# Node stage of a four-layer graph network: the row means leave two products with gamma

## The chip, the cores and the metric

The kernel runs on one core of one Trainium2 chip. The metric is the time of one execution on the device, in microseconds; the median of three runs is shown below. Engines are named as the profile names them: PE (TensorE), DVE (VectorE), ACT (ScalarE), POOL (GpSimd), SP (SyncE).

## What is computed

50,000 nodes with 128 features go through four layers, each followed by a residual and a layer norm. Edges (25,000) are sorted by their destination. What bears on this change is the dense work that every node gets, edge or no edge. In the first layer a node without edges only sees itself, so its row is

```python
out = x @ W + bias
f = gelu(out)
f = (f - mean(f)) / sqrt(var(f) + 1e-5) * gamma + beta     # gamma, beta: L0
x1 = layernorm(x + (f + x))
```

and in the third layer (L2) a node without incoming edges has no message, so that

```python
h = x2 + bo                                                # x2: a layer-normed row
h = (h - mean(h)) / sqrt(var(h) + 1e-5) * gamma + beta     # gamma, beta: L2
x3 = layernorm(x2 + h)
```

All of it is float32. Nodes with edges are computed again in later stages ("hops") and written over the others.

## The kernel before, in words

The program is a row of stages with a barrier of all engines between them. Setup loads the weights and derives small tables. Then comes the **node stage**, which the change is about: it takes all nodes through the layers as if they had no edges. After it come the marks of the edges' ends, the hops of the four layers, and a copy of the result.

The node stage takes 1,024 nodes per iteration: 49 chunks, and 57 turns of a loop over `t`, since a chunk is worked on over eight turns (software pipelining). Chunk `t` is loaded, turned, multiplied with `W0` and gone through gelu; chunk `t-1` gets its first layer norm and residual; `t-2` its second norm; `t-3` the second layer's three products; `t-4` and `t-5` the third norm; `t-6` and `t-7` the third layer. Tiles are 128 partitions wide and hold 8 rows of 128 features per partition (128x1024), worked on in two halves (`h` = 0 and 1, four rows of 128 each, 128x512). The same turn also takes 512 edges' end points through a gather (POOL), two turns on PE and a store.

Each engine runs its own list of instructions, in the order in which the code is written, and waits on semaphores; there is no scheduler. So what a wait holds up is everything written behind it on its engine. Names that matter:

- `gelu(c, h)` on ACT (L604) writes `gT[h]`, the gelu rows with the features on the partitions. `turn_g(c, h)` on PE turns them by `turn` (L368, four transposes with `ident`) into the PSUM tiles `T_G[h]`, rows on the partitions.
- DVE takes statistics of a row by `bn_stats` (L694, "stats"), two rows to an instruction. Once per turn a **batch** of ten small instructions (L716 to L769, tiles of 40 columns) makes from all rows' variances the factors `rs` = 1/sqrt(var + eps) and `nm` = -mean * rs, for the five norms at once. Its last (L769) signals `scaled`.
- Between the batch's small instructions lie the wide ones: L719 adds a bias to `xw_b[2]`, the last tile that ACT copies in a turn (L686, signal `xw2`); L724, L732, L767 and the stats of the third norm follow.
- Behind `scaled`, DVE works on the first norm: L782 makes `a_b = (T_G - mean) * gamma0`, one instruction for each of the 8 rows, since the mean is a number per partition and row; L786 makes `t_b = a_b * rs + t_b`, again a row at a time. Then the stats of `t_b`; L794 `hd_b = x2 + bo` and its stats; stats of `T_G[0]`; L804 makes `d_b = (hd_b - mean) * gamma2` in 8 instructions and L808 `s_b = d_b * rs + s_b` in 8; stats of `s_b` and of `T_G[1]`.
- ACT waits for `scaled` at its L626 and then runs its three sets of eight `apply` instructions (L594, 128x128 each, for the second, third and fifth norm), two gelus, four relus and the copies out of PSUM, down to L686.

The lines of DVE around the change:

```python
V.scalar_tensor_tensor(out=blocks(a_b)(4 * h + k), in0=blocks(T_G[h])(k), scalar=mean[:, LNA, 4 * h + k:4 * h + k + 1],
                       in1=gamma0[:], op0=ALU.subtract, op1=ALU.mult).then_inc(S("ag"), 1)
...
V.scalar_tensor_tensor(out=blocks(d_b)(k), in0=blocks(hd_b[q % 2])(k), scalar=mean[:, LND, k:k + 1],
                       in1=gamma2[:], op0=ALU.subtract, op1=ALU.mult).then_inc(S("dg"), 1)
```

Of the kernel before, what the change touches and what calls it, by code (L numbers as in the profile page):

```python
# [47 lines left out]
def build(nc, x, src, dst, ea32, ea64, ew, w, out):  # L48
# [3 lines left out]
    def sb(name, shape, dt=F32):  # L52
        return ctx.enter_context(nc.sbuf_tensor(name, shape, dt))
# [43 lines left out]


    ident = sb("ident", [P, P])
    ones = sb("ones", [1, P])  # L100
    eps = sb("eps", [P, 1])
    W0 = sb("W0", [P, D])
# [41 lines left out]
    with ExitStack() as tmp:  # L144
# [7 lines left out]
        att = tb("att", [P, 2, D])  # L152
        prod = tb("prod", [P, 4, D])
        sums = tb("sums", [P, 6, 4])
        Win, WinT, Ws0 = tb("Win", [P, D]), tb("WinT", [P, D]), tb("Ws0", [P, D])
        b_in_rep = tb("b_in_rep", [P, P])
        b_in, bs0c = tb("b_in", [P, 1]), tb("bs0c", [P, 1])
# [28 lines left out]
        with nc.Block() as block:  # L186
# [66 lines left out]
            @block.vector  # L253
            def _(v):
                V = nc.vector
                v.wait_ge(pool_dma["edges"], 64)
                V.tensor_copy(edge_f[:], edge_i[:]).then_inc(S("edges_f"), 1)
                v.wait_ge(S("edges_f"), 1)

                V.tensor_tensor(mark[:, :, 0, :], edge_f[:, :, 1, :], edge_f[:, :, 3, :], ALU.is_equal).then_inc(S("m"), 1)  # L260
                V.tensor_tensor(mark[:, :, 1, :], edge_f[:, :, 1, :], edge_f[:, :, 2, :], ALU.is_equal).then_inc(S("m"), 1)
                v.wait_ge(S("m"), 2)
                V.tensor_scalar(mark[:, :, 4, :], mark[:, :, 0, :], float(FAR), None, ALU.mult).then_inc(S("m"), 1)
                V.tensor_scalar(mark[:, :, 2, :], mark[:, :, 1, :], 0.5, 2 * BIG / 2, ALU.subtract, ALU.mult).then_inc(S("marks"), 1)
                v.wait_ge(S("m"), 3)
                V.tensor_tensor(mark[:, :, 3, :], mark[:, :, 4, :], edge_f[:, :, 1, :], ALU.add).then_inc(S("marks"), 1)

                v.wait_ge(S("win_ps"), 1)
                V.tensor_copy(b_in_rep[:], b_in[:, 0:1].to_broadcast([P, P])).then_inc(S("b_rep"), 1)
                v.wait_ge(S("b_rep"), 1)  # L270
                V.tensor_copy(WinT[:], ps[:, 0, 0:P]).then_inc(S("winT"), 1)
                v.wait_ge(S("wi0_ps"), 3)
                V.tensor_copy(xw0_bias[:], ps[:, 5, 0:P])
                V.tensor_copy(WI0[:], ps[:, 0, 128:256])
                V.tensor_tensor(h1_bias[:], ps[:, 0, 384:385], bs0c[:], ALU.add)
                V.tensor_tensor(prod[:, 0, :], W0[:], att[:, 0, :], ALU.mult).then_inc(S("prod"), 1)
                V.tensor_tensor(prod[:, 1, :], W0[:], att[:, 1, :], ALU.mult).then_inc(S("prod"), 1)
                v.wait_ge(S("prod"), 2)
                for k, t in enumerate((prod[:, 0, :], prod[:, 1, :], Wq3[:], Wk3[:])):
                    V.tensor_reduce(sums[:, k, :], t.rearrange("p (h c) -> p h c", h=4), AX.X, ALU.add).then_inc(S("sums"), 1)  # L280
                V.tensor_reduce(We3s[0:64, :], We3[:].rearrange("p (h c) -> p h c", h=4), AX.X, ALU.add).then_inc(S("sums"), 1)
                v.wait_ge(S("sums"), 5)
                V.memset(att_src[:, 4:8], 0.0)
                V.tensor_copy(att_src[:, 0:4], sums[:, 0, :])
                V.tensor_copy(att_dst[:, 0:4], sums[:, 1, :])
                V.tensor_tensor(att_dst[:, 4:8], sums[:, 0, :], sums[:, 1, :], ALU.add)
                V.tensor_copy(q3_cols[:], sums[:, 2, :])
                V.tensor_copy(k3_rep.rearrange("p (h c) -> p h c", h=4), by_row(sums[:, 3, :], 32))
                V.tensor_copy(we3_rep[0:64, :].rearrange("p (h c) -> p h c", h=4),
                              We3s[0:64, :, None].to_broadcast([64, 4, 32]))  # L290
                V.tensor_scalar(we3_rep[64:65, :].rearrange("p (h c) -> p h c", h=4),
                                We3s[64:65, :, None].to_broadcast([1, 4, 32]), float(32.0 ** 0.5), None, ALU.mult)
                V.tensor_copy(we2_rep.rearrange("p (h c) -> p h c", h=8), We2[:, :, None].to_broadcast([33, 8, 16]))

                v.wait_ge(S("cols_ps"), 6)
                v.wait_ge(S("zeros"), 7)
                V.tensor_copy(src_idx[:, 0:TILES], ps[:, 1, 0:TILES])
                V.tensor_copy(dst_idx[:, 0:TILES], ps[:, 2, 0:TILES])
                V.tensor_copy(end_idx[:, 0:TILES], ps[:, 3, 0:TILES])
# [93 lines left out]
    def wide_rows(t):  # L393

        return t.rearrange("p (j f) -> p j f", f=D)
# [5 lines left out]
    with ExitStack() as tmp:  # L401
# [33 lines left out]
        with nc.Block() as block:  # L435
# [66 lines left out]
            def _(pe):  # L502
# [15 lines left out]
                def turn_g(c, h):  # L518
                    pe.wait_ge(S("gelu"), 2 * c + h + 1)
                    if c:  # L520
                        pe.wait_ge(S("ag"), 8 * (c - 1) + 4 * h + 4)
                    turn(pe, T_G[h], gT[h]).then_inc(S("g_ps"), 1)

                def scores(k):
                    pe.wait_ge(S("xsT"), k + 1)
# [163 lines left out]
            def _(v):  # L689
# [14 lines left out]
                v.wait_ge(S("raw"), 2)  # L704
                for t in range(N_CH + 8):
                    of = raw[(t - 1) % 2].rearrange("p n k (r s) -> p (n k r) s", r=2)
                    mean = raw[(t - 1) % 2].rearrange("p n k (r s) -> p n (k r) s", r=2)[:, :, :, 1]
                    r, b = rs[t % 2].rearrange("p n k -> p (n k)"), nm[t % 2].rearrange("p n k -> p (n k)")
                    n0 = 10 * t
                    cw, cv, cw2 = t - 1, t - 4, t - 6  # L710
# [61 lines left out]
                    for h in range(2):  # L772
                        if m:
                            v.wait_ge(S("xw0_ps"), 2 * c + h + 1)
                            if h == 0 and c >= 2:
                                landed(v, "xw0_out", 2, c - 2)
                            V.tensor_tensor(rows4(half(xw_b[0][c % 2], h)), rows4((T_D, T_B)[h]), each_row(xw0_bias), ALU.add).then_inc(S("xw0"), 1)
                        if live(a):
                            v.wait_ge(S("scaled"), t + 1)
                            v.wait_ge(S("w"), a + 1)  # L780
                            for k in range(4):
                                V.scalar_tensor_tensor(out=blocks(a_b)(4 * h + k), in0=blocks(T_G[h])(k), scalar=mean[:, LNA, 4 * h + k:4 * h + k + 1],  # L782
                                                       in1=gamma0[:], op0=ALU.subtract, op1=ALU.mult).then_inc(S("ag"), 1)
                            for k in range(4 * h, 4 * h + 4):
                                v.wait_ge(S("ag"), 8 * a + k + 1)
                                V.scalar_tensor_tensor(out=blocks(t_b[a % 2])(k), in0=blocks(a_b)(k), scalar=rs[t % 2][:, LNA, k:k + 1],  # L786
                                                       in1=blocks(t_b[a % 2])(k), op0=ALU.mult, op1=ALU.add).then_inc(S("t"), 1)
                            if h == 1:
                                v.wait_ge(S("t"), 8 * a + 8)
                                stats(LNB, t, pairs(t_b[a % 2]), 0, 4, "b_st")  # L790
                    if live(t - 5):
                        q = t - 5
                        v.wait_ge(S("x2"), 2 * (q + 1))
                        V.tensor_tensor(wide_rows(hd_b[q % 2][:]), wide_rows(x2_b[q % 3][:]), row_of_all(bo), ALU.add).then_inc(S("hd"), 1)  # L794
                        v.wait_ge(S("hd"), q + 1)
                        stats(LND, t, pairs(hd_b[q % 2]), 0, 4, "d_st")
                    if live(t):
# [2 lines left out]
                    if live(t - 6):  # L800
                        q = t - 6
                        v.wait_ge(S("w2"), q + 1)
                        for k in range(8):
                            V.scalar_tensor_tensor(out=blocks(d_b)(k), in0=blocks(hd_b[q % 2])(k), scalar=mean[:, LND, k:k + 1],  # L804
                                                   in1=gamma2[:], op0=ALU.subtract, op1=ALU.mult).then_inc(S("dg"), 1)
                        for k in range(8):
                            v.wait_ge(S("dg"), 8 * q + k + 1)
                            V.scalar_tensor_tensor(out=blocks(s_b[q % 2])(k), in0=blocks(d_b)(k), scalar=rs[t % 2][:, LND, k:k + 1],  # L808
                                                   in1=blocks(s_b[q % 2])(k), op0=ALU.mult, op1=ALU.add).then_inc(S("s"), 1)
                        v.wait_ge(S("s"), 8 * q + 8)  # L810
                        stats(LNE, t, pairs(s_b[q % 2]), 0, 4, "e_st")
# [1339 lines left out]
```

## Time and profile before

| | us |
|---|---|
| three runs | 4228.57, 4228.95, 4229.52 |
| median | 4228.95 |
| the profiled execution's own time | 4232.34 |
| span of that execution (first to last instruction) | 4230.3 |
| node stage in it, from L769 of the first turn to the next stage | 29.4 to 1285.4 |
| busy in the span: DVE, PE, POOL, ACT | 3478, 2900, 2568, 2509 |
| mean granted TensorE clock, share of 2.4 GHz | 0.738 |

The profile is of one execution. Busy time counts when an engine had an instruction in work; waits on semaphores are not in it. Instructions that follow each other on an engine overlap a little in the trace, so a group of four may span less than four durations; what counts on a path is the distance from start to start. A row of the timeline merges neighbours that are alike: "x8" with its start and the time from the first start to the last end. Square brackets behind a row tell the idle time before it and what ended it.

### The profile page before, as it was taken

The numbers are of one execution on the slowest core, as the hardware profiler recorded it, in microseconds if no ns is written. First come the engines' busy times: TensorE is split into PE (matmuls) and PEld (weight loads), VectorE is DVE, ScalarE is ACT, GpSimd is POOL, SyncE is SP. The second block draws the span as 40 slices with busy tenths as digits, with TensorE's granted clock in tenths as the row PEclk, the third lists the DMA queues.
The fourth block names the chain that finished last, engine by engine and source line by source line (L and its number), as shares of the span: only waits on it lengthen the run. The fifth ranks groups of instructions, "written<-read, shape, count | busy, mean of one in ns | idle before, by whom it ended". The sixth has DMA issues, their size and how long they took to land. (4 is left out here: it accounts for less than half of the span.)

```text
span 4230.3 us, 49000 instructions
## 1 busy us (share of the span) xinstructions
PE 2899.9 (69%) x12128; PEld 1933.6 (46%) x12128; DVE 3478.3 (82%) x8156; ACT 2509.0 (59%) x5535; POOL 2568.4 (61%) x2300
## 2 busy tenths in 40 slices
PE   5877777777742788745465455478888885777775
PEld 3555455554530344444455344345555554444443
DVE  4999999999986888668788699677777785788886
ACT  3777777777751666635545444356666564565555
POOL 6666666666501666167577577587666651666664
PEclk9899999999975777667657655677777785655655
DMA  4887766665534888457667566322222221333331
GB/s 117 182 184 192 188 180 193 183 192 188 174 138 122 253 249 254 150 176 245 220 199 242 196 184 198 94 73 69 64 66 66 69 55 38 102 87 91 91 94 49
DMA packets 390823, 624.83 MB, mean 148 GB/s; under 512 B 125015, under 2 KB 206080, under 8 KB 390542
## 3 DMA queue, kind: packets, MB, share of 16 engines
q1 hardware_dynamic: 320782, 508.68, 40.0%
q0 software_dynamic: 69760, 113.02, 11.4%
q8 instruction: 101, 1.65, 0.2%
q14 instruction: 180, 1.47, 0.1%
HBM read 338.14 MB, written 287.17 MB: 148 GB/s over the span
## 5 line engine op out<-in xcount | busy, mean ns | idle before, releaser
L1563 POOL DMA_INDIRECT gs_g<-table_xw,slot_idx x588 | 616.8, 1049 | 319.5 <-issue 261.9
L886 POOL DMA_INDIRECT gs_t<-table_x,slot_idx x392 | 418.4, 1067 | 302.3 <-issue 198.9
L493 POOL DMA_INDIRECT gs<-x,src_idx x200 | 223.9, 1119 | 292.2 <-DMA xd_rows<-gd 211.0
L368 PE MATMUL ps<-ident,gs_g 128*128 128x128 f32 x588 | 143.4, 391 | 369.1 <-DMA gs_g<-table_xw,slot_idx 369.0
L1258 POOL DMA_INDIRECT slot_idx<-node_map,src_idx x200 | 242.1, 1211 | 196.9 <-DMA slot_idx<-node_map,src_idx 103.6
L481 POOL DMA_INDIRECT node_map<-slot_no,end_idx x200 | 302.6, 1513 | 60.9 <-issue 60.0
L1601 ACT ACTIVATE hT_g<-u_g 128x512 f32<-128x512 f32 x147 | 92.4, 629 | 391.5 <-DVE u_g L1662 391.1
L1828 POOL DMA_INDIRECT out<-x_t,end_idx x196 | 205.5, 1049 | 169.4 <-ACT x_t L339 116.7
L368 PEld LDWEIGHTS ps<-ident,gs_g 128*128 128x128 f32 x588 | 95.9, 200 | 408.0 <-issue 344.6
L1655 DVE TENSOR_TENSOR_SCAN agg_g<-same_seg,agg_g,ps 128x512 f32<-128x512 uint8 x147 | 187.8, 1278 | 93.1 <-PE ps L368 92.5
L493 POOL DMA_INDIRECT gd<-x,dst_idx x200 | 218.7, 1093 | 60.9 <-issue 59.7
L1887 PE MATMUL ps<-xsT_t,Wv 128*128 128x512 f32 x196 | 156.1, 890 | 132.3 <-DVE msg_t L939 132.1
L886 POOL DMA_INDIRECT own_t<-table_x,own_idx x196 | 200.9, 1025 | 59.7 <-issue 59.7
L1650 DVE SCALAR_TENSOR_TENSOR own_g<-bs_row,root,own_g 128x128 f32<-128x128 f32 x588 | 166.7, 345 | 27.6 <-DMA own_g<-table_xw 26.7
L1979 ACT COPY xsT_t<-ps 128x512 f32<-128x512 f32 x49 | 28.7, 585 | 249.3 <-PE ps L368 249.3
L374 PE MATMUL ps<-WS,hT_g 128*128 128x128 f32 x784 | 163.1, 378 | 9.6 <-ACT xw_g L1609 9.3
L594 ACT ACTIVATE x_b<-v_b,nm,rs 128x128 f32<-128x128 f32 x392 | 156.6, 495 | 17.1 <-DVE nm L769 17.1
L368 PE MATMUL ps<-ident,own_g 128*128 128x128 f32 x588 | 146.5, 398 | 29.0 <-DVE own_g L1650 28.0
L594 ACT ACTIVATE x_b<-s_b,nm,rs 128x128 f32<-128x128 f32 x392 | 156.7, 496 | 14.1 <-DVE nm L769 14.1
L374 PEld LDWEIGHTS ps<-WS,hT_g 128*128 128x128 f32 x784 | 154.9, 293 | 11.8 <-issue 11.2
L1952 ACT COPY xsT_t<-ps 128x512 f32<-128x512 f32 x98 | 56.4, 576 | 172.8 <-PE ps L368 172.8
L594 ACT ACTIVATE x_b<-t_b,nm,rs 128x128 f32<-128x128 f32 x392 | 157.4, 510 | 0.0
(365 smaller groups left out, 9936.3 us busy)
## 6 DMA issues: line engine op xcount, KB each, us to landing
table_xw<-xw_b SPq DMA_DIRECT2D x147, 512.0 KB, 4.6
table_x<-x_b SPq DMA_DIRECT2D x98, 512.0 KB, 2.8
own_g<-table_xw SPq DMA_DIRECT2D x147, 256.0 KB, 4.2
x_in<-x SPq DMA_DIRECT2D x49, 512.0 KB
y_g<-table_x SPq DMA_DIRECT2D x49, 512.0 KB, 4.8
table_xw<-xw_g SPq DMA_DIRECT2D x98, 256.0 KB, 2.8
out<-y_g SPq DMA_DIRECT2D x49, 512.0 KB, 4.2
pen_t<-pen_row SPq DMA_DIRECT2D x98, 256.0 KB, 4.1
```

Of the source, the lines that this page charges most:

```text
L368: last = nc.tensor.transpose(to[0:width, j * P:(j + 1) * P], t[:, j * width:(j + 1) * width], ident[:])
L374: last = nc.tensor.matmul(to[:, j * D:(j + 1) * D], tT[:, j * P:(j + 1) * P], W[:], start=True, stop=bias_row is None)
L481: pool.indirect_dma_start(out=node_map, out_offset=bass.IndirectOffsetOnAxis(ap=end_idx[:, t:t + 1], axis=0), in_=slot_no[:, t:t + 1], in_ ...
L493: pool.indirect_dma_start(out=to[k % 3][:, j * D:(j + 1) * D], out_offset=None, in_=x, in_offset=bass.IndirectOffsetOnAxis(ap=of[:, n:n + ...
L594: last = nc.scalar.activation(to[:, k * D:(k + 1) * D], of(k), ACT.Identity, scale=r[:, n, k:k + 1], bias=b[:, n, k:k + 1])
L886: pool.indirect_dma_start(out=self.B[L % RING][g][:, t * D:(t + 1) * D], out_offset=None, in_=table, in_offset=bass.IndirectOffsetOnAxis(a ...
L1258: pool.indirect_dma_start(out=slot_idx[:, t:t + 1], out_offset=None, in_=node_map, in_offset=bass.IndirectOffsetOnAxis(ap=src_idx[:, t:t + ...
L1563: pool.indirect_dma_start(out=gs[c % 6][:, j * D:(j + 1) * D], out_offset=None, in_=tables[layer], in_offset=bass.IndirectOffsetOnAxis(ap= ...
L1650: V.scalar_tensor_tensor(out=blk, in0=bs_row[layer][:], scalar=root4[:, k:k + 1], in1=blk, op0=ALU.mult, op1=ALU.add).then_inc(S("own_bias ...
L1655: V.tensor_tensor_scan(agg[t % 3][:], same_seg[:, t * CH:(t + 1) * CH], T_X[t % 2], agg[(t - 1) % 3][:, CH - 1:CH], ALU.mult, ALU.add).the ...
L1828: pool.indirect_dma_start(out=out, out_offset=bass.IndirectOffsetOnAxis(ap=end_idx[:, k:k + 1], axis=0), in_=B[L % RING]["x4"][:, t * D:(t ...
L1887: nc.tensor.matmul(K[3], (Wv if kind == 2 else Wv3)[:], B[L % RING]["xsT"][:], start=True, stop=True).then_inc(S("v_ps"), 1)
```

## The change

Neither product with gamma has a mean in it any more.

- Setup makes two more constants: `centre` = `ident` - 1/128, so that a row times `centre` is the row less its mean; and `bo_c` = `bo` less its own mean. This adds three instructions on DVE (one subtraction ahead of its wait for `win_ps`; a sum over `bo` and a multiply-add behind that wait), with a wait between the last two.
- `turn_g` no longer transposes with `ident` but multiplies: `rows_times` (L374 before; four float32 products of 128x128) with `gT[h]` as the stationary side and `centre` as the moving one. `T_G` then holds the gelu rows with their means taken off.
- L782's four instructions per half become one `tensor_tensor` of 128x512 (`T_G * gamma0`), and L786's four wait for it as a whole.
- `hd_b` is made with `bo_c`. `x2` is a layer-normed row, so its mean is zero up to rounding, and so is that of `hd_b`. L804's eight instructions become one `tensor_tensor` of 128x1024 (`hd_b * gamma2`), and L808's eight wait for it as a whole.
- `turn_g`'s wait on `ag` counts 1 per half instead of 4; it still means that DVE has read the tile of the turn before.

Nothing changes its place in an engine's order.

```diff
     ident = sb("ident", [P, P])
+    centre = sb("centre", [P, P])
+    bo_c = sb("bo_c", [P, D])
...
+        bo_sum = tb("bo_sum", [P, 1])
...
+                v.wait_ge(S("masks"), 5)
+                V.tensor_scalar(centre[:], ident[:], 1.0 / D, None, ALU.subtract).then_inc(S("centre"), 1)
                 v.wait_ge(S("win_ps"), 1)
+                V.tensor_reduce(bo_sum[:], bo[:], AX.X, ALU.add).then_inc(S("bo_sum"), 1)
+                v.wait_ge(S("bo_sum"), 1)
+                V.scalar_tensor_tensor(out=bo_c[:], in0=bo_sum[:, 0:1].to_broadcast([P, D]), scalar=-1.0 / D, in1=bo[:],
+                                       op0=ALU.mult, op1=ALU.add).then_inc(S("bo_c"), 1)
                 V.tensor_copy(b_in_rep[:], b_in[:, 0:1].to_broadcast([P, P])).then_inc(S("b_rep"), 1)
...
                 def turn_g(c, h):
                     pe.wait_ge(S("gelu"), 2 * c + h + 1)
                     if c:
-                        pe.wait_ge(S("ag"), 8 * (c - 1) + 4 * h + 4)
-                    turn(pe, T_G[h], gT[h]).then_inc(S("g_ps"), 1)
+                        pe.wait_ge(S("ag"), 2 * (c - 1) + h + 1)
+                    rows_times(pe, T_G[h], gT[h], centre).then_inc(S("g_ps"), 1)
...
-                            for k in range(4):
-                                V.scalar_tensor_tensor(out=blocks(a_b)(4 * h + k), in0=blocks(T_G[h])(k), scalar=mean[:, LNA, 4 * h + k:4 * h + k + 1],
-                                                       in1=gamma0[:], op0=ALU.subtract, op1=ALU.mult).then_inc(S("ag"), 1)
+                            V.tensor_tensor(rows4(half(a_b, h)), rows4(T_G[h]), each_row(gamma0), ALU.mult).then_inc(S("ag"), 1)
+                            v.wait_ge(S("ag"), 2 * a + h + 1)
                             for k in range(4 * h, 4 * h + 4):
-                                v.wait_ge(S("ag"), 8 * a + k + 1)
                                 V.scalar_tensor_tensor(out=blocks(t_b[a % 2])(k), in0=blocks(a_b)(k), scalar=rs[t % 2][:, LNA, k:k + 1],
                                                        in1=blocks(t_b[a % 2])(k), op0=ALU.mult, op1=ALU.add).then_inc(S("t"), 1)
...
-                        V.tensor_tensor(wide_rows(hd_b[q % 2][:]), wide_rows(x2_b[q % 3][:]), row_of_all(bo), ALU.add).then_inc(S("hd"), 1)
+                        V.tensor_tensor(wide_rows(hd_b[q % 2][:]), wide_rows(x2_b[q % 3][:]), row_of_all(bo_c), ALU.add).then_inc(S("hd"), 1)
...
+                        V.tensor_tensor(wide_rows(d_b[:]), wide_rows(hd_b[q % 2][:]), row_of_all(gamma2), ALU.mult).then_inc(S("dg"), 1)
+                        v.wait_ge(S("dg"), q + 1)
                         for k in range(8):
-                            V.scalar_tensor_tensor(out=blocks(d_b)(k), in0=blocks(hd_b[q % 2])(k), scalar=mean[:, LND, k:k + 1],
-                                                   in1=gamma2[:], op0=ALU.subtract, op1=ALU.mult).then_inc(S("dg"), 1)
-                        for k in range(8):
-                            v.wait_ge(S("dg"), 8 * q + k + 1)
                             V.scalar_tensor_tensor(out=blocks(s_b[q % 2])(k), in0=blocks(d_b)(k), scalar=rs[t % 2][:, LND, k:k + 1],
                                                    in1=blocks(s_b[q % 2])(k), op0=ALU.mult, op1=ALU.add).then_inc(S("s"), 1)
```

## Rows read from the trace of the kernel before

**Rows 1.** Windows: stretch, length, busy PE, PEld, DVE, ACT, POOL, PEclk, DMA share, GB/s

```profile
165.78:1176.94 1011.16, 774.56 (x4022) 526.97 (x4022) 998.55 (x2941) 767.02 (x1721) 639.30 (x502) 0.91 0.69 186
```

**Rows 2.** Timeline of DVE, one full turn: start us, us, line, operation

```profile
671.43 0.20 DVE L769 SCALAR_TENSOR_TENSOR nm<-raw,rs 128x40 f32<-128x40 f32 x1
671.54 0.68 DVE L777 TENSOR_TENSOR xw_b<-ps,xw_bias 128x512 f32<-128x512 f32 x1
672.14 1.11 DVE L782 SCALAR_TENSOR_TENSOR a_b<-ps,raw,gamma 128x128 f32<-128x128 f32 x4
673.17 1.13 DVE L786 SCALAR_TENSOR_TENSOR t_b<-a_b,rs,t_b 128x128 f32<-128x128 f32 x4
...
678.36 1.21 DVE L794 TENSOR_TENSOR hd_b<-x_b,bo 128x1024 f32<-128x1024 f32 x1
...
681.60 2.17 DVE L804 SCALAR_TENSOR_TENSOR d_b<-hd_b,raw,gamma 128x128 f32<-128x128 f32 x8
683.69 2.18 DVE L808 SCALAR_TENSOR_TENSOR s_b<-d_b,rs,s_b 128x128 f32<-128x128 f32 x8
...
688.14 1.22 DVE L719 TENSOR_TENSOR h_b<-xw_b,bs_row 128x1024 f32<-128x1024 f32 x1
...
695.45 0.20 DVE L769 SCALAR_TENSOR_TENSOR nm<-raw,rs 128x40 f32<-128x40 f32 x1
```

**Rows 3.** Timeline of ACT in the same turn

```profile
671.66 0.69 ACT L626 ACTIVATE h1T<-ps,h_bias 128x512 f32<-128x512 f32 x1 [4.65 <-DVE nm L769]
...
673.85 3.20 ACT L594 ACTIVATE x_b<-v_b,nm,rs 128x128 f32<-128x128 f32 x8
...
687.17 0.61 ACT L686 COPY xw_b<-ps 128x512 f32<-128x512 f32 x1
...
695.69 0.69 ACT L626 ACTIVATE h1T<-ps,h_bias 128x512 f32<-128x512 f32 x1 [4.66 <-DVE nm L769]
```

**Rows 4.** Waits of DVE, 100 to 1180: us in total, times, longest

```profile
DVE h_b L719 <- ACT xw_b L686: 6.1, 5, 3.0
```

**Rows 5.** Timeline of PE in the turn of rows 2

```profile
673.36 1.05 PE L374 MATMUL ps<-WS,h1T 128*128 128x128 f32 x8
674.25 0.60 PE L368 MATMUL ps<-ident,gT 128*128 128x128 f32 x4
...
681.80 0.74 PE L368 MATMUL ps<-ident,gT 128*128 128x128 f32 x4 [2.97 <-ACT gT L604]
...
683.19 1.91 PE L374 MATMUL ps<-WS,h2T 128*128 128x128 f32 x8
...
687.45 1.02 PE L527 MATMUL ps<-xsT,att_src 128*8 128x512 f32 x2 [1.58 <-ACT xdT L683]
```

**Rows 6.** Timeline of PE at the head of another, late turn

```profile
592.56 1.91 PE L528 MATMUL ps<-xdT,att_dst 128*8 128x512 f32 x2
```

**Rows 7.** Windows around that head, columns as in rows 1

```profile
589.00:597.00 8.00, 6.10 (x13) 2.47 (x14) 7.83 (x21) 4.46 (x10) 5.03 (x4) 0.51 0.80 199
597.00:605.00 8.00, 8.00 (x47) 5.74 (x46) 7.93 (x27) 5.21 (x12) 5.21 (x5) 1.00 0.62 129
```

**Rows 8.** Timeline of ACT in that late turn

```profile
599.16 0.69 ACT L626 ACTIVATE h1T<-ps,h_bias 128x512 f32<-128x512 f32 x1 [2.17 <-DVE nm L769]
...
602.11 1.26 ACT L594 ACTIVATE x_b<-v_b,nm,rs 128x128 f32<-128x128 f32 x3
```

**Rows 9.** Timeline of DVE in setup

```profile
19.08 0.23 DVE L269 COPY b_in_rep<-b_in 128x128 f32<-128x128 f32 x1 [7.86 <-PE ps L242]
...
21.38 0.29 DVE L273 COPY xw_bias<-ps 128x128 f32<-128x128 f32 x1 [1.74 <-PE ps L246]
```

**Rows 10.** Timeline of PE in the second turn of the loop

```profile
54.81 1.12 PE L368 MATMUL ps<-ident,gs 128*128 128x128 f32 x4 [6.62 <-DMA gd<-x,dst_idx]
```

**Rows 11.** Timeline of ACT in the fifth turn

```profile
106.97 0.69 ACT L604 ACTIVATE gT<-ps,bias_col 128x512 f32<-128x512 f32 x1 [0.71 <-PE ps L516]
```

**Rows 12.** Timeline of DVE in a turn near the stage's end

```profile
1223.34 1.22 DVE L794 TENSOR_TENSOR hd_b<-x_b,bo 128x1024 f32<-128x1024 f32 x1 [2.69 <-ACT x_b L594]
```

More of the change, by code:

```diff
@@ L706, in _ @@
                     of = raw[(t - 1) % 2].rearrange("p n k (r s) -> p (n k r) s", r=2)
-                    mean = raw[(t - 1) % 2].rearrange("p n k (r s) -> p n (k r) s", r=2)[:, :, :, 1]
                     r, b = rs[t % 2].rearrange("p n k -> p (n k)"), nm[t % 2].rearrange("p n k -> p (n k)")
```

## Prediction

> **What bounds the kernel now.** I read the stages first. The node stage has 57 turns of its loop, and 42 of them are full turns that lie between 165.78 and 1176.94: 1011.16 us, so 24.07 us each [rows 1]. DVE is busy 998.55 us of that, 98.8%; ACT has 767, PE 775, POOL 639. Read by shares, the stage is DVE's, and whatever DVE is spared comes off the time. The other stages are untouched by the change.
>
> Then I read one full turn engine by engine, because a share does not tell how close the second limit is. DVE runs from the end of L769 at 671.63 to the end of the next at 695.65 without a gap [rows 2]: 24.02 us. In the same turn ACT starts on L626 at 671.66, 0.03 us behind the end of L769, and its last copy (L686) ends at 687.17 + 0.61 = 687.78 [rows 3]. Between the two ACT has no idle time in the timeline. It is a chain of its own, 16.12 us long. DVE's L719 reads what L686 wrote; it starts at 688.14, 0.36 us after the copy's end. The waits of DVE list only five turns of 45 in which L719 waited for L686 [rows 4]; two of the five lie at the start of the stage and make most of the 6.1 us. So there is a **second loop**: L769 releases ACT, ACT ends with L686, L686 releases L719, and from L719 to the end of the next L769 DVE needs 695.65 - 688.14 = 7.51 us. Its length, with 0.03 us for each hand-over, is 0.03 + 16.12 + 0.03 + 7.51 = **23.69 us**. It is 0.33 us shorter than the turn. This number decides the forecast, since nothing that the change takes off DVE lies between L719 and L769.
>
> **The change, part by part.**
>
> *d, 8 instructions to 1.* From the start of L804 to that of L808 is 2.09 us [rows 2]. The new instruction has the form of L794 (128x1024, a row spread over eight), 1.21 us, and L808 now waits for all of it, another 0.03. Saved: 0.85 us of DVE.
>
> *a, 4 to 1, twice.* From L782 to L786 is 1.03 us [rows 2]. The new form is that of L777 (128x512 out of PSUM with a row spread over four): 0.68 us, with the hand-over 0.71. Saved: 0.32 us, twice. Together DVE has **1.49 us less** per turn, and 22.5 us of work.
>
> *What of it comes off the turn.* The two loops run together, and the longer sets the pace: 23.69 by ACT, 22.5 by DVE. A full turn gets 0.33 us shorter, and DVE waits some 1.2 us at L719 in each. Three of the 42 turns ran by ACT's loop already (the other three waits of rows 4) and gain nothing. 39 x 0.33 = 12.9 us.
>
> *Other waits of DVE that it now reaches earlier.* L794 waits for ACT's first set of eight, which ends at 673.85 + 3.20 = 677.05 [rows 3]; DVE comes there at 678.36 - 0.64 = 677.72 [rows 2]. It stays free by 0.67 us.
>
> *turn_g by a product.* Four blocks as L374 take 1.05 us, four transposes 0.60 [rows 5]: 0.45 us more for each half at the full clock. At the lower clock L374 takes 1.91 [rows 5], which makes the added time up to 0.9. What waits on it in a full turn? Behind the second half stand the turn of the gathered rows and then the product that L686 copies; it ended at 683.19 + 1.91 = 685.10 and ACT comes for it at 687.17 [rows 3, 5], 2.07 us later. Even 0.9 us fits. PE itself has gaps before `turn_g` (2.97) and before the scores (1.58) [rows 5]. I cost it at nothing in full turns, under cover of these gaps; were they gone, it would be 2 x 0.45 per turn.
> The Trainium skill ("Perfetto Trace Analysis", Transposes) says that a logical transpose should be done as a transpose and not as a standard matmul, because it has logic that skips the arithmetic. The trace agrees on the price, 0.60 against 1.05 us; if the price lay on the path, 98 halves would add 44 us to the sum.
>
> *The stage's ends.* In the turn before the 42 ACT had less to do, so DVE's full 1.49 comes off. Of the last seven turns, in five DVE's chain runs through d with no other wait behind it, as after 1223.34, where L794 waits for ACT and d follows [rows 12]: 0.85 each, 4.2 us. At the head, the second and third turns are paced by the gathers (PE waits 6.62 us for one at 54.81 [rows 10]), so longer turns of PE do not add up there; in the fifth, ACT waits for a product behind `turn_g` [rows 11], and 0.45 us more shows.
>
> *Setup.* The subtraction stands before a wait of 7.86 us [rows 9] and costs nothing. The sum and the multiply-add stand behind it, on a path through PE back to DVE (the next wait is for PE too [rows 9]). Neither form is in the trace of this tile; they can't be below zero, and two 128x128 instructions that wait for each other are, by the copies of 0.23 and 0.29 us [rows 9], about 0.5 and under 1. I take 0.5.
>
> **Sum**: 12.9 + 1.5 + 4.2 = 18.6 off, 0.45 + 0.5 = 1.0 on, so 17.6 us off. Against the profiled execution, 4232.3, this gives 4214.7; the median of the runs is 3.4 below that execution, so the forecast is **4211.5**. Its own range is 4207 to 4217: the three turns of ACT's loop may be none or ten, and the ends may give half or all.
>
> **Rivals.**
>
> *A. All of DVE's saving comes through.* ACT's chain would have to shrink with DVE's. 42 x 1.49 + 1.5 + 4.2 - 1.0 = 67 us off: 4161. For it: DVE at 98.8%, and ACT idle a fifth of the turn. Against it: that idle time is ACT's wait for L769, 4.65 us [rows 3], which is part of the loop; and in the turns of rows 4 DVE did wait. Chance 0.03.
> The Trainium skill ("Perfetto Trace Analysis", Identifying the Most-Contended Engine) would have the engine with the highest occupancy be optimized first; by that rule alone 4161 is the forecast. The row on shares agrees that it is DVE.
>
> *B. PE's clock eats the gain.* In the late turn of rows 6 to 8 PE ran at 0.51 of 2.4 GHz, its level of 1.2, for eight microseconds, after a pause in which it waited for ACT [rows 7]; two records took 1.91 instead of 1.02 us [rows 5, 6]. Then the copy `xT` in ACT's chain waited for PE, and from L626 to the first L594 it took 2.95 instead of 2.19 us [rows 3, 8]: 0.76 more. Before, 0.33 of that was hidden; now all of it counts. With n such turns more than the three, the sum is 17.6 less 0.76 n: twelve bring it within 0.2%, 23 to nothing. For it: the head of a turn has 0.33 us less slack, and PE has more to do. Against it: the work is added in front of the very pauses after which the clock fell, and the mean clock is 0.91 [rows 1]. With 12 to 30 such turns the time is 4220 to 4234. Chance 0.17.
>
> *C. Slower: every turn at the lower clock at its head.* The mechanism of B in all 39 turns, because the new period of 23.7 us lets the low stretch fall on the head each time, or because PE's longer turns make ACT wait. The place is ACT's `xT` copy (L600) and the price 0.76 a turn, 30 us: 4241. It decides above zero from 23 turns. Nothing in the trace repeats like that. Chance 0.05.
>
> *D. The change does more than the sum says, by half.* Were some of ACT's instructions shorter with DVE idle beside them, by 0.01 us for each of 40, the loop would lose 0.4 us: 4195. I see no row for it. Chance 0.05.
>
> **Numbers.** Forecast 0.70, A 0.03, B 0.17, C 0.05, D 0.05. The bound between same and different is 0.2%, 8.5 us, about what a measurement of this kernel can tell. Faster by more: forecast, A, D, less a little of the forecast's upper edge, 0.77; within 0.2%: 0.18; slower: 0.05. The range from 4200 to 4226 takes the forecast and most of B, and leaves out A, C and the ends of B and D.
>
> **What would show it.** Right: the full turns at 23.7 us; in the waits of DVE, L719 waiting for L686 in about 40 turns, some 1.2 us each; DVE's busy share in the stretch down to about 95%; ACT's chain still 16.12 us; turn_g's rows with eight records and about 1.05 us; L600 waiting in few turns. The theory of the second loop is wrong if the turn falls below 23.6, or if L719 does not wait. The size is wrong if L719 waits but the turn is over 23.8; then L600's waits tell whether it was B.

## The result, and the profile after

| | before | changed |
|---|---|---|
| median of 20 runs each, us | 4228.61 | 4216.78 |
| the profiled execution, us (span) | 4232.34 (4230.3) | 4215.43 (4213.5) |
| ratio | | 0.9972, 95% interval 0.9964 to 0.998 |
| mean granted TensorE clock | 0.738 | 0.745 |

The ratio makes 11.8 us, with an interval from 8.5 to 15.2; the forecast was 17.5. The time lies within the range, and the interval of the ratio ends just at 0.2%. Two runs of the changed kernel (4588 and 9203 us) and one of the kernel before (8675 us) were slow, and the ratio leaves them out. The other 19 runs of the kernel before lie between 4215.8 and 4238.5; the three shown ahead of the prediction agreed within 1 us by chance.

So the pair of profiled executions, 16.8 us apart in span, can't be read as the effect of the change. I took the ends of the stages from both traces. The node stage, from ACT's first instruction to POOL's first of the next stage, went from 1259.1 to 1250.1 us: **9.0 us less**. The stages behind it hold the same instructions in both and took 2944.8 and 2936.6 us. Over the two kernels and eight others below, whose stages behind the node stage are all the same, that part took from 2932 to 2945. It varies by itself, so the 8.2 us by which the two differ there say nothing of the change.

Windows of the changed kernel; the line answers to [rows 1], the 42 full turns (columns as there):

```profile
167.40:1171.50 1004.10, 798.89 (x4355) 524.28 (x4356) 936.81 (x2396) 771.26 (x1721) 578.55 (x503) 0.93 0.67 187
```

DVE has 62 us less work, as the sum said (42 x 1.49), and its share fell from 98.8% to 93.3%. PE has 24 us more. The stretch got only 7.1 us shorter, where the forecast had 12.9. In the mean a turn takes 23.91 us instead of 24.07; the median turn takes 23.89 us instead of 24.03, where the forecast had 23.69.

DVE in one full turn, which answers to [rows 2]:

```profile
645.65 0.20 DVE L777 SCALAR_TENSOR_TENSOR nm<-raw,rs 128x40 f32<-128x40 f32 x1
...
646.37 0.68 DVE L789 TENSOR_TENSOR a_b<-ps,gamma 128x512 f32<-128x512 f32 x1
647.08 1.14 DVE L792 SCALAR_TENSOR_TENSOR t_b<-a_b,rs,t_b 128x128 f32<-128x128 f32 x4
...
651.97 1.22 DVE L800 TENSOR_TENSOR hd_b<-x_b,bo_c 128x1024 f32<-128x1024 f32 x1
...
655.23 1.21 DVE L809 TENSOR_TENSOR d_b<-hd_b,gamma 128x1024 f32<-128x1024 f32 x1
656.47 2.19 DVE L812 SCALAR_TENSOR_TENSOR s_b<-d_b,rs,s_b 128x128 f32<-128x128 f32 x8
...
660.81 0.19 DVE L724 TENSOR_SCALAR big<-raw 128x40 f32<-128x40 f32 x1
662.22 1.23 DVE L727 TENSOR_TENSOR h_b<-xw_b,bs_row 128x1024 f32<-128x1024 f32 x1 [1.23 <-ACT xw_b L695]
```

The prices are right: a in 0.71 us from start to start (647.08 - 646.37), d in 1.24. And the wait is where it was expected: L727, the old L719, stands for 1.23 us behind ACT's last copy. Over the stage, the waits of DVE, which answer to [rows 4]:

```profile
DVE h_b L727 <- ACT xw_b L695: 55.1, 43, 2.8
```

The window of this row is 100 to 1160: 43 waits, 55 us in all. In the 42 full turns alone it waits in every one, 51.1 us together. What was freed on DVE became this wait. Now ACT, which answers to [rows 3]:

```profile
645.89 0.69 ACT L635 ACTIVATE h1T<-ps,h_bias 128x512 f32<-128x512 f32 x1 [2.77 <-DVE nm L777]
...
647.04 0.69 ACT L640 ACTIVATE h1T<-ps,h_bias 128x512 f32<-128x512 f32 x1
647.78 0.59 ACT L609 COPY xT<-ps 128x512 f32<-128x512 f32 x1
648.26 3.19 ACT L603 ACTIVATE x_b<-v_b,nm,rs 128x128 f32<-128x128 f32 x8
...
661.11 0.60 ACT L692 COPY xdT<-ps 128x512 f32<-128x512 f32 x1
661.58 0.61 ACT L695 COPY xw_b<-ps 128x512 f32<-128x512 f32 x1
```

From L635 (the old L626) to the end of L695 (the old L686) it is 661.58 + 0.61 - 645.89 = 16.30 us, where 16.12 was expected. The difference lies in front of L609, the copy `xT` of the second half: it starts 0.74 us behind L640, not 0.57 as its neighbours do. It waits for PE. PE at the head of this turn, later in it, and at the head of the next, which answers to [rows 5]:

```profile
637.96 1.87 PE L536 MATMUL ps<-xsT,att_src 128*8 128x512 f32 x2 [2.73 <-ACT xdT L692]
...
647.14 0.60 PE L377 MATMUL ps<-ident,x_in 128*128 128x128 f32 x4
...
649.33 1.06 PE L383 MATMUL ps<-centre,gT 128*128 128x128 f32 x8
...
656.20 1.16 PE L383 MATMUL ps<-centre,gT 128*128 128x128 f32 x8 [1.88 <-ACT gT L613]
...
661.86 1.86 PE L536 MATMUL ps<-xsT,att_src 128*8 128x512 f32 x2 [2.73 <-ACT xdT L692]
663.52 1.79 PE L537 MATMUL ps<-xdT,att_dst 128*8 128x512 f32 x2
665.24 1.09 PE L377 MATMUL ps<-ident,x_b 128*128 128x128 f32 x8
```

The product in `turn_g` costs what it should (1.06 against 0.60 us). But the two products of the scores take 1.8 us each, where they took 1.02 [rows 5]. Windows on this place, 2.6 us long, in three turns that lie ten turns apart:

```profile
662.20:664.80 2.60, 2.60 (x4) 0.27 (x2) 2.54 (x4) 0.47 (x1) 1.80 (x2) 0.50 0.78 224
901.20:903.80 2.60, 2.60 (x4) 0.28 (x2) 2.56 (x4) 0.40 (x1) 1.72 (x2) 0.50 0.71 235
1140.20:1142.80 2.60, 2.60 (x4) 0.27 (x2) 2.57 (x4) 0.34 (x1) 0.31 (x1) 0.50 0.71 246
```

The granted clock there is 0.50, the level of 1.2 GHz, in each. I read the same place in all 42 full turns: the mean granted clock over the 2.6 us from the start of the scores is 0.60 in the first and 0.50 to 0.59 in all others. In the kernel before the scores ran at or near the lower clock in 18 of the 42 turns.

### The profile page after: what moved, and what is told of

It reads as the page before. It is cut to its first block and busy times, and to the rows that moved or that the text cites. A ratio compares the mean times of both kernels' runs of the same rounds, so it can differ in the third digit from the quotient of the medians.

```text
span 4213.5 us, 49150 instructions
## 1 busy us (share of the span) xinstructions
PE 2925.4 (69%) x12520; PEld 1933.7 (46%) x12520; DVE 3406.1 (81%) x7522; ACT 2511.9 (60%) x5535; POOL 2507.0 (59%) x2300
## 5 line engine op out<-in xcount | busy, mean ns | idle before, releaser
L377 PE MATMUL ps<-ident,gs_g 128*128 128x128 f32 x588 | 139.9, 384 | 353.7 <-DMA gs_g<-table_xw,slot_idx 353.4
L502 POOL DMA_INDIRECT gd<-x,dst_idx x200 | 253.3, 1267 | 60.9 <-issue 60.0
L377 PEld LDWEIGHTS ps<-ident,gs_g 128*128 128x128 f32 x588 | 93.3, 195 | 392.7 <-issue 329.4
L490 POOL DMA_INDIRECT node_map<-slot_no,end_idx x200 | 212.1, 1061 | 61.0 <-issue 60.4
L377 PE MATMUL ps<-ident,own_g 128*128 128x128 f32 x588 | 148.0, 401 | 44.2 <-DVE own_g L1654 43.6
L1983 ACT COPY xsT_t<-ps 128x512 f32<-128x512 f32 x49 | 28.7, 585 | 245.3 <-PE ps L377 245.3
L536 PE MATMUL ps<-xsT,att_src 128*8 128x512 f32 x100 | 85.9, 958 | 126.7 <-ACT xdT L692 126.7
L383 PE MATMUL ps<-centre,gT 128*128 128x128 f32 x784 | 110.9, 286 | 81.6 <-ACT gT L613 81.5
L603 ACT ACTIVATE x_b<-v_b,nm,rs 128x128 f32<-128x128 f32 x392 | 156.2, 484 | 15.2 <-DVE nm L777 15.2
```

The lines of the kernel that those rows point to most:

```text
L377: last = nc.tensor.transpose(to[0:width, j * P:(j + 1) * P], t[:, j * width:(j + 1) * width], ident[:])
L383: last = nc.tensor.matmul(to[:, j * D:(j + 1) * D], tT[:, j * P:(j + 1) * P], W[:], start=True, stop=bias_row is None)
L490: pool.indirect_dma_start(out=node_map, out_offset=bass.IndirectOffsetOnAxis(ap=end_idx[:, t:t + 1], axis=0), in_=slot_no[:, t:t + 1], in_ ...
L502: pool.indirect_dma_start(out=to[k % 3][:, j * D:(j + 1) * D], out_offset=None, in_=x, in_offset=bass.IndirectOffsetOnAxis(ap=of[:, n:n + ...
L603: last = nc.scalar.activation(to[:, k * D:(k + 1) * D], of(k), ACT.Identity, scale=r[:, n, k:k + 1], bias=b[:, n, k:k + 1])
```

## The experiments

The theory that came out of this reading, L in the expectations: a **third loop** sets the pace. When ACT's copy `xdT` (L692) ends, PE's scores start 0.15 us later, at the lower clock (L536, at 637.96 in this turn). PE works down to the turn of the second half of x (L377, `x_in`), which ends at 647.74, 9.78 us behind that start. 0.04 us later ACT copies it (L609, 647.78). From there ACT needs 13.93 us without a gap to the end of the next L692 at 661.71. 0.15 + 9.78 + 0.04 + 13.93 = 23.90 us, and each step starts when the one before it ends. With the scores at 2.4 GHz the PE part was 8.2 us (687.45 to 695.65 in the trace before) and the loop 22.3, out of sight. The 1.6 us between the two is the scores alone (3.39 us from their start to what follows them, against 1.81 before); the rest of PE's part takes 6.39 us in both. The rival, P: the longer `turn_g` is what PE is late by.

All kernels below are compared with the kernel before, run beside them. The ratios of the changed kernel (0.9964 to 0.998) and of the two runs with a move of PE's step or a filled gap below overlap, so those are told apart by their full turns, 42 in one trace each, and not by their times. Where the time of a turn is given, it is the median over the 42 full turns, from the end of one last small instruction of the batch to the next.

### The DVE part alone

This kernel has the change's list of instructions on DVE and the transposes of the kernel before on PE. It leaves out the means of the first layer's product.

```diff
-                    rows_times(pe, T_G[h], gT[h], centre).then_inc(S("g_ps"), 1)
+                    turn(pe, T_G[h], gT[h]).then_inc(S("g_ps"), 1)
```

> The changed kernel with turn_g again as four transposes with ident, so the means are left out of the first layer's product and its rows are wrong by them; DVE's list is that of the change. In the changed kernel's trace a full turn lasts 23.89 us instead of the 23.69 that I forecast. Theory L: a third loop sets it, from ACT's copy xdT (L692) over PE's scores at the lower clock to the turn of the second half of x and ACT's copy xT (L609), and turn_g is not in it. Then a full turn is 23.85 to 23.92 here too, and the time is that of the change, 4214 to 4220. Theory P: the longer turn_g on PE costs those 0.2 us. Then a full turn is 23.69 and the time about 4208.

Measured: ratio 0.9972 (0.9959 to 0.9984), median 4215.1. A full turn takes 23.89 us, the 42 together 1003.1. The clock at the head of a turn:

```profile
660.40:663.00 2.60, 2.60 (x4) 0.27 (x2) 2.33 (x2) 0.69 (x2) 2.02 (x2) 0.50 0.61 206
```

ACT stands before its copy `xT` as in the changed kernel:

```profile
645.46 0.69 ACT L640 ACTIVATE h1T<-ps,h_bias 128x512 f32<-128x512 f32 x1
646.20 0.58 ACT L609 COPY xT<-ps 128x512 f32<-128x512 f32 x1
```

P falls: with four transposes in place of the products the turn is the same to 0.01 us. The product on PE costs nothing in the full turns, and the low clock at the head is not its doing.

### The PE part alone

```diff
+    centre = sb("centre", [P, P])
...
+                v.wait_ge(S("masks"), 5)
+                V.tensor_scalar(centre[:], ident[:], 1.0 / D, None, ALU.subtract).then_inc(S("centre"), 1)
...
-                    turn(pe, T_G[h], gT[h]).then_inc(S("g_ps"), 1)
+                    rows_times(pe, T_G[h], gT[h], centre).then_inc(S("g_ps"), 1)
```

> The kernel before with turn_g as a product with centre and the subtraction in setup; DVE still subtracts a mean, which is now zero, in 8 and 8 instructions. Theory L: DVE sets the turn at 24.02 us as before, and the product lies under PE's gaps: full turns 24.02 to 24.05, the stage's first five turns together about 1 us longer, time 4229 to 4231. Theory P: full turns 24.1 to 24.3, time 4233 to 4241.

Measured: ratio 0.9999 (0.9986 to 1.0011), median 4227.3; a full turn 24.03 us. The product lies under PE's gaps, as the forecast had it. Within its interval the time is that of the kernel before.

### One step of PE moved, out of the third loop

```diff
                         nc.tensor.matmul(T_A, WI0[:], x1T[1][:], start=True, stop=True).then_inc(S("h1_ps"), 1)
-                        rows_times(pe, T_B, x1T[1], WI0).then_inc(S("xw0_ps"), 1)
                     if f:
                         turn_x(t, 1)
+                    if m:
+                        rows_times(pe, T_B, x1T[1], WI0).then_inc(S("xw0_ps"), 1)
```

> The changed kernel with one step of PE moved: the turn of the second half of x (T_XT) comes before the four products of the second layer's first rows (T_B) instead of behind them, 0.89 us sooner. Theory L: the third loop gets 0.89 us shorter, from 23.89 to 23.0, and the loop by L686 and L719 takes over: full turns 23.69 to 23.72, ACT's chain 16.13 again, 42 x 0.2 = 8 us less than the change, 4208. Theory P: no difference to the change.

Measured: ratio 0.9958 (0.9946 to 0.9971), median 4207.5; a full turn 23.73 us, the 42 together 997.0, 7.1 less than in the changed kernel. The low clock still comes to the scores, in whole or in part in 20 of the 42 turns, as in this one:

```profile
655.89 1.44 PE L536 MATMUL ps<-xsT,att_src 128*8 128x512 f32 x2 [2.73 <-ACT xdT L693]
657.13 1.91 PE L537 MATMUL ps<-xdT,att_dst 128*8 128x512 f32 x2
...
664.24 0.60 PE L377 MATMUL ps<-ident,x_in 128*128 128x128 f32 x4
```

But the turn of x comes sooner behind the scores, and `xT` no longer waits (0.57 us from L641 to L610):

```profile
665.22 0.69 ACT L641 ACTIVATE h1T<-ps,h_bias 128x512 f32<-128x512 f32 x1
665.79 0.59 ACT L610 COPY xT<-ps 128x512 f32<-128x512 f32 x1
```

A move of four transposes past four products changes no work at all and gives what the loop said. With the lower clock at the scores the loop is now 0.15 + 8.95 + 0.04 + 13.93 = 23.07 us, below the 23.69 of the second loop, and turns with and without the low clock there last the same 23.7 us. That is theory L's own test, and it holds.

### The gap ahead of the scores filled

```diff
+                    if m and c:
+                        pe.wait_ge(S("xw1"), 2 * c)
+                        for _ in range(10):
+                            nc.tensor.matmul(T_B[:, 0:P], ident[:], ident[:], start=True, stop=True)
                     if edge(t - 1):
                         scores(t - 1)
```

> The changed kernel with ten more products of 128x128 on PE ahead of the scores (ident by ident into T_B, whose last reader is done), some 2.2 us in the gap of 2.7 us in which PE waits for xdT. Nobody reads them. Theory L: what makes the third loop as long as 23.89 is that the scores and what follows run 3.4 us at 1.2 GHz behind that gap. Without the gap the granted clock stays at 1.0 at the head of a turn, the two scores take 1.02 us each instead of 1.8, and a full turn is 23.69: 4208. If the clock falls in spite of the products, the turn stays at 23.89 or gets longer, up to 24.1, by products that run on into the scores. Theory P: 23.89 or more whatever the clock does.

Measured: ratio 0.9964 (0.995 to 0.9977), median 4207.1; a full turn 23.72 us, the 42 together 996.6. PE, with the ten products at L547:

```profile
657.15 2.54 PE L547 MATMUL ps<-ident 128*128 128x128 f32 x20
659.62 1.03 PE L536 MATMUL ps<-xsT,att_src 128*8 128x512 f32 x2
660.48 1.02 PE L537 MATMUL ps<-xdT,att_dst 128*8 128x512 f32 x2
```

and the clock at the head:

```profile
662.00:664.60 2.60, 2.36 (x15) 1.65 (x14) 2.50 (x11) 1.19 (x3) 0.00 (x0) 1.00 1.17 225
```

The scores take 1.0 us each again. In this trace useless work makes the 42 turns 7.5 us shorter than in the changed kernel: the granted clock is 1.00 at the scores in all of them, and the loop that passes there is out of sight again. The Trainium skill ("TensorE: Matmul & The Clock Gate", HAM oscillation) says that pauses of PE between bursts of work bring the clock down and that the next burst starts at half rate; this pair of traces agrees, 1.8 us for a score behind a pause of 2.73 us against 1.03 us for the same product without it.

### ACT's set for the second norm behind the copies

```diff
-                    if live(t - 2):
-                        q = t - 2
-                        if q >= 3:
-                            act.wait_ge(S("v"), q - 2)
-                        for h in range(2):
-                            apply(LNB, x1_b[q % 3], lambda k: t_b[q % 2][:, k * D:(k + 1) * D], r, b, h, "b_out")
...
                     if m:
                         act.wait_ge(S("xw2_ps"), 2 * c + 2)
                         nc.scalar.copy(half(xw_b[2][c % 2], 1), T_A).then_inc(S("xw2"), 1)
+                    if live(t - 2):
+                        q = t - 2
+                        if q >= 3:
+                            act.wait_ge(S("v"), q - 2)
+                        for h in range(2):
+                            apply(LNB, x1_b[q % 3], lambda k: t_b[q % 2][:, k * D:(k + 1) * D], r, b, h, "b_out")
```

> The changed kernel with ACT's eight instructions of the second norm (x1_b, 3.09 us) moved behind the three copies of a turn's end, so that L686's successor, for which DVE waits, comes 3.09 us sooner. If ACT's chain is what holds back the rest of DVE's saving, DVE sets the turn again, at 24.02 - 1.48 = 22.54 us: 42 x 1.35 = 57 us less than the change, about 4159, and DVE no longer waits at the bias of xw_b. Rival: the pace was DVE's and PE's together, or the moved set makes PE wait for x1_b at the head of a turn; then full turns stay above 23 us, and the time above 4180.

Measured: ratio **0.986** (0.9833 to 0.9887), median 4168.4; a full turn 22.65 us in the median, the 42 together 957.2, 47 less than in the changed kernel. The waits of DVE:

```profile
DVE t_b L740 <- ACT x_b L603: 5.7, 14, 0.5
...
DVE xw_b L785 <- PE ps L383: 3.4, 8, 0.8
DVE h_b L727 <- ACT xw_b L689: 1.9, 2, 1.0
```

The 55 us of waiting for ACT's last copy have gone to 1.9, and those two waits lie ahead of the 42 full turns. DVE sets the pace: 24 of the turns last 22.5 to 22.7 us, where 22.54 was expected. Of the 57 us expected, 47 came: 15 turns last 22.9 to 23.3 us, where DVE now meets other waits (L740 for the moved set, L785 for PE). The waits that the view lists in the 42 turns add up to 6.0 us of the missing 10. ACT around the head of one such turn (the two last copies are L686 and L689 in this kernel), and windows on the clock just ahead of the first and the third row:

```profile
659.04 0.59 ACT L686 COPY xdT<-ps 128x512 f32<-128x512 f32 x1 [1.02 <-PE ps L377]
660.24 0.59 ACT L689 COPY xw_b<-ps 128x512 f32<-128x512 f32 x1 [0.61 <-PE ps L383]
...
672.13 0.59 ACT L609 COPY xT<-ps 128x512 f32<-128x512 f32 x1 [0.64 <-PE ps L377]
```

```profile
657.00:659.00 2.00, 2.00 (x11) 2.00 (x11) 1.97 (x8) 1.02 (x3) 1.49 (x2) 0.50 1.00 377
667.00:669.00 2.00, 2.00 (x8) 1.48 (x8) 1.97 (x8) 0.00 (x0) 0.00 (x0) 0.50 0.83 107
```

The granted clock is 0.50, the lower level, in both windows, and ACT waits for PE behind them: 1.02, 0.61 and 0.64 us. That the lower clock is the cause of the long turns was not tried in this kernel.

### The same move in the kernel before

The edit is the diff of the section above, made in the kernel before.

> The kernel before with the same move of ACT's set. There DVE set the turn, with 0.33 us to spare in ACT's loop: full turns stay at 24.0 us, and the time at 4227 to 4229. Only the few turns that ran by ACT's loop gain, 1.4 us in all, and a few at the stage's head. Rival: the move is worth something by itself, also without the change: then the time is below 4220.

Measured: ratio 0.9992 (0.9981 to 1.0002), median 4224.2; a full turn 24.02 us. In 17 of the 42 full turns ACT's chain is 13.06 or 13.07 us, 3.06 us shorter, and DVE reads its end 3.4 us later; in the others ACT waits for PE inside it, it is up to 14.45 us long, and 2.0 us are still left. The pace does not move: the 42 turns together went from 1011.2 to 1010.0 us. The first seven went from 136.4 to 134.0 and the last seven from 103.0 to 102.5. So in the full turns the move is worth 1 us without the change; with it, the two are worth 59 us in the median (the run above), of which the change alone brings 12.

### Half of the change on DVE: a alone

```diff
+                    mean = raw[(t - 1) % 2].rearrange("p n k (r s) -> p n (k r) s", r=2)[:, :, :, 1]
...
-                        V.tensor_tensor(wide_rows(d_b[:]), wide_rows(hd_b[q % 2][:]), row_of_all(gamma2), ALU.mult).then_inc(S("dg"), 1)
-                        v.wait_ge(S("dg"), q + 1)
                         for k in range(8):
+                            V.scalar_tensor_tensor(out=blocks(d_b)(k), in0=blocks(hd_b[q % 2])(k), scalar=mean[:, LND, k:k + 1],
+                                                   in1=gamma2[:], op0=ALU.subtract, op1=ALU.mult).then_inc(S("dg"), 1)
+                        for k in range(8):
+                            v.wait_ge(S("dg"), 8 * q + k + 1)
```

> The changed kernel with the product d as before, in 8 instructions with the mean; of DVE's saving only the part of a is left, 0.64 us a turn. By the two loops 0.33 us is all that can be had: full turns are those of the change, 23.72 to 23.9, since DVE alone would need 23.38; only the last turns lose 0.85 each, 4 us: time 4219 to 4221. Rival: the saving counts by its size: full turns 0.85 us longer than in the change or half of what it gained, 24.0, and the time 4224.

Measured: ratio 0.9978 (0.9966 to 0.999), median 4215.5; a full turn 23.90 us, the 42 together 1002.9, the last seven 103.0 against 99.6 in the changed kernel. The waits of DVE:

```profile
DVE h_b L728 <- ACT xw_b L695: 19.0, 43, 2.8
```

Less than half of the saving gives the same turn; the other 0.85 us a turn is the difference between this wait (19 us) and that of the changed kernel (55). The median of the runs came out lower than expected, by less than its interval.

### Both moves

The changed kernel with ACT's set moved and PE's step moved, both diffs as above.

> The changed kernel with both moves, ACT's set behind the copies and PE's turn of the second half of x 0.89 us sooner. If DVE alone sets the turn once ACT's set is moved, the second move adds nothing: 22.54 us a turn, 4159. If the loop by PE at the lower clock is still close, it is a few us faster than the first move alone.

Measured: ratio 0.9849 (0.9828 to 0.9871), median 4165.3; a full turn 22.67 us, the 42 together 958.9. No difference to the one move that can be told from the spread.

### Two second looks

The changed kernel and the kernel before again, with no edit.

> The changed kernel once more, for a second profile. If the pace of 23.89 us and the place of the low clock are a steady state of the loop by PE, the full turns are 23.89 again in the second half of the stage, within 0.03. If they were an accident of one execution, the median of the full turns lies anywhere from 23.7 to 24.2. The first five turns tell how much that part differs from execution to execution: 94.2 us in the first profile; by 1 us or more would mean that the 2.5 us by which they were longer than in the kernel before can't be laid to the change.

> The kernel before once more, for a second profile. Full turns 24.02 again, first five turns 91.7 us in the first profile; the stages behind the node stage took 2945 us there and 2937 in the changed kernel, which are the same instructions. If that difference is one from execution to execution, they come out 3 us or more away from 2945 here or away from 2937 in the other run.

Inconclusive for what they were meant to show. The two executions took 4490 and 4537 us and one of the kernel before beside them 4561, 6 to 8% over the others. In the changed kernel's profile POOL waited 402 us for the DMA behind its gathers in the node stage, full turns took up to 29 us, and the stages behind took 3094 us where the ten others have 2932 to 2945. In neither profile did the turns keep their usual pace for long, and none of the changed kernel's settled at 23.89 us. One thing can be read from it: 21 of its 42 full turns began with the scores at a granted clock of 1.00. Of these, 13 lasted 23.71 to 23.77 us, and the other eight, held up further, 24.3 to 26.8. So without the low clock at its head the changed kernel's own turn can be close to the 23.69 us of the second loop. What the others show of the first five turns stands below.

## Why the prediction was right, and where it was off

The sum of the forecast against the two profiles, term by term:

| term | forecast, us | measured, us |
|---|---|---|
| DVE's work in a full turn | -1.49 | -1.49 |
| the 42 full turns | -12.9 | -7.1 |
| the turn ahead of them | -1.5 | -1.35 |
| the last seven turns | -4.2 | -3.4 |
| the fifth turn | +0.45 | +0.47 |
| the first four turns | 0 | +2.1 |
| setup | +0.5 | +0.43 |
| setup and node stage together | -17.6 | -8.6 |

**The second loop was right.** DVE's saving did not come off the time; it became the wait at L719. The waits and the prices say so, and the experiments bound it from both sides: less than half of the saving gives as much (a alone), and most of it comes once ACT's chain is cut (the set moved: 54 us of the 63 in the 42 turns, counted from the kernel before).

**The step that failed** is the term of the full turns, -12.9 us, which measured -7.1. The prediction had named the sign: the size is wrong if L719 waits but the turn is over 23.8, and it was 23.89. The failure is in "turn_g by a product", where the prediction asked what waits for PE. It looked at what stands behind `turn_g` and found 2 us to spare, which was right. It did not ask the same of the head of the turn, whose PE chain at 2.4 GHz had 1.76 us to spare before ACT's `xT` copy (695.65 to 697.41). The scores at the lower clock take 1.6 us of that, and the shorter turn takes 0.33; for the sum it took the higher clock for given. Rival B named the place and the wait, but as an event of single turns at 0.76 us each, and rival C, that the new period could put the low stretch on the head of every turn, got 0.05. It is C's mechanism that happened, at a quarter of its price: 0.2 us a turn, not 0.76, because the low stretch covers the scores there, and not all of the PE chain. So the full turns were mis-sized: 7.1 us over 42 turns are 0.17 off each, where the sum had 0.31 (12.9 over 42).

**The last turns** fell short by 0.8 us of 4.2: in one of them, of 20.8 us, ACT waited 0.6 us for PE. With the gap filled that turn takes 20.1 us, as in the kernel before, and the last seven 98.85, which is the 4.2 of the forecast.

**The first four turns** were forecast as paced by the gathers. They were 2.1 us longer. In the sums of the first five turns the product is not shown to be the cause: the DVE part alone, which has no product, has its first five turns at 93.9 us, the changed kernel 94.2, the PE part alone 93.8, PE's step moved 92.1, the kernel before 91.7. The kernel with a alone has 93.7, the one with the gap filled 94.7. This stayed open; the two second looks that were meant for it were disturbed.

**What was luck.** Setup and node stage together missed the forecast by 9.0 of 17.6 us: 5.8 in the full turns, 2.1 in the first four, 0.8 in the last seven, 0.3 in small ones. The medians missed by only 5.3, since they show 11.8 us where the stage accounts for 8.6. That difference lies within the interval of the ratio (8.5 to 15.2), and the stages behind, with their own spread from 2932 to 2945 us, hold nothing of the change. With 8.6 us the change is worth 0.2% and hardly more. (The forecast's own terms give 4211.3, not 4211.5: 4214.7 less 3.4.)

**The rivals.** A (all of DVE's saving comes through, 4161) was wrong for this kernel and came close for the one with ACT's set moved: 4168. The Trainium skill's rule ("Perfetto Trace Analysis", Identifying the Most-Contended Engine), weighed there, pointed at the engine whose share was highest; here a chain through ACT, which was 76% busy, was 0.33 us behind it, and the trace went with the chain. B's price of 0.76 us and its single turns did not come: the low clock at the head came in every turn and cost less. D did not happen. The Trainium skill's rule on transposes ("Perfetto Trace Analysis", Transposes) was no matter here: 98 products in place of 98 sets of transposes left the time at 0.9999 of what it was (the PE part alone).

Both ranges of the forecast (4207 to 4217 and 4200 to 4226) hold the result, the narrow one by 0.2 us; the best guess was 5.3 us low.

## What to carry to other kernels

Before an engine at 99% is relieved, follow the loop that its signal closes through the other engines and back, and compare its length with the turn: the gain ends at the difference, here 0.33 of 1.49 us. Then look for the instruction that the loop passes without need; eight instructions on ACT that nobody was waiting for yet stood in front of the copy that DVE waited for, and moving them was worth 47 us where the change had been worth 12. A chain through PE has two lengths, one for each level of its clock (here 8.2 and 9.8 us), and the slack must be counted at the lower.

## What the runs showed that had not been expected

**The loop and the low clock fall into step.** In the changed kernel, in the DVE part alone and in a alone, three kernels with different work on PE and DVE, the full turn came out at 23.89, 23.89 and 23.90 us, and the low stretch stood at the scores in every full turn. It took some turns to get there: the first full turn lasts 23.71 or 23.72 us in each. In the kernel before, at 24.03 us, the place of the low stretch wanders: it stood at the scores in 18 of the 42 turns, and only three turns were held up by it. Each of the three kernels has one such trace; the disturbed second look at the changed kernel did not fall into step, so how often an execution does is not known. Why the pace settles just there was not tried; what was tried is that it goes with the low clock (gap filled: 23.72) and with the chain that it lengthens (step moved: 23.73).

**Ten products that nobody reads** made the 42 full turns 7.5 us shorter, as much as a reordering (7.1).

**Runs.** One profile each of two kernels can differ by 8 us in stages that hold the same instructions. A change of 0.3% is better read from the turns of its own stage than from a pair of spans.
